# Slot bias carried inside the logits weights, slot sums moved to ScalarE and GpSimd, and the first combine weights split among the experts

## The chip, the cores and the metric

One core of a Trainium2 chip runs the whole program. The metric is the device time in microseconds from start to end of one execution, as a median of several runs. Matrices are multiplied by TensorE (PE, with its weight load PEld), the other engines are VectorE (DVE), ScalarE (ACT), GpSimd (POOL) and SyncE (SP), which issues most of the DMAs.

## What is computed

The reference, cut to what matters:

```python
h = patches @ W.T + b                       # 32 images, 36 patches each, 256 channels
h = concatenate([h, txt], axis=1)           # 36 + 77 = 113 tokens an image, 3616 in all
h = h + attention(layernorm(h))             # 16 heads of 16, rotary q and k, no scale or shift in the norm
x = layernorm(h)                            # mean 0 over the 256 channels
logits = (x @ phi_w.T + phi_b).reshape(t, z, 64, 32)      # 64 experts, 32 slots each: 2048 columns
D, C = softmax(logits, axis=3), softmax(logits, axis=2)   # dispatch and combine weights
X = einsum('tznp,tzd->npd', D, x)           # slot sums over all tokens
X = tanh(normalise(clip(X)))
Y = einsum('npd,ndH->npH', X, expert_w) + expert_b
out = h + einsum('tznp,npH->tzH', C, Y)
```

All is float32. Products that need care are made as three products of a high part and a low part: `hi*hi + hi*lo + lo*hi`.

## The kernel before

The program has three parts, one after the other, with a barrier of all engines between them.

**`embed`** multiplies 9 tiles of 128 patches by the patch weights on PE. Meanwhile ACT loads the weights of the later parts, and ACT and POOL split them into high and low parts (L126, L133): `wqk`, `wv`, `wo`, and last and largest `phi`, the slot weights (128 x 4096 elements), of whose low part DVE makes one half (L170). DVE also makes `bias_rows` from the slot bias, broadcast to 64 partitions: the bias in row 0, its low part in row 32, zeros elsewhere (L152 to L165).

**`attend`** goes over the 32 images as a software pipeline. Each engine runs `step(b)` for b = -3 to 33: the step normalises image b+3, projects b+2, turns b+1, scores b, and finishes b-1 and b-2. On POOL a step is the reciprocal standard deviation of the next image (L383, L385) and the sums that finish the rotary turn (L395). ACT's step ends with `xt_hi` of the next image (L447). SP loads `h_in` ahead and stores `h2`.

**`slots`** goes over 29 tiles of tokens (one of 32 rows, then 28 of 128), `step(t)` for t = -2 to 28: t up to 4 written out, 5 to 20 in a loop of 8 steps, the rest written out. What matters of a step, engine by engine:

- PE: turns `xn` of tile t+1 (L1068), makes two units of slot sums (`add_products`, L1092: for a group of four tiles, two blocks of 128 slots a unit) in `p_sum`, turns the combine weights of tile t-1 in four quarters (L1083), and makes the logits of tile t+1 in four banks of 512 columns: a bias product of `bias_ones` and `bias_rows` (L1115) and six products (L1118). In steps 5 and later the units come first and the banks are woven between the quarters; in steps up to 4 all four banks come before the units.
- DVE: per bank of the logits a maximum (L811) and a subtraction (L816), the sum of the combine weights of tile t-1 (L800), `xt_lo` (L828), the combine maximum (L839), the end of the norm (L784), the dispatch sum (L845), and then `keep_sum`: the two units of `p_sum` are copied (first group, L792) or added (L794) into `xacc`.
- ACT: copies the four banks to `comb` (L1004), takes the exponentials of `disp` and `comb` (L989), and copies the turned quarters out of PSUM (L978).
- POOL: the deviation of a later tile (L922, L924), two subtractions on `comb` that wait for L839 (L929), the scaling of `disp` (L933), which waits for L845's reciprocal, and the scaling of `comb` of the same tile (L937), which waits for L800's reciprocal, made by DVE one step later.

After the last tile PE makes eight more units (`products`), DVE adds them and normalises (`gather`, `scale`), ACT takes tanh, PE turns the blocks and applies the experts (L1167), DVE adds the expert bias (L879), ACT and POOL split the result (L1031, L951). Then `combine` runs over the 29 tiles: the stored combine weights are split (ACT L1057, DVE L904) and multiplied in 48 products a tile (L1200). The first combine product waits for `lo` of tile 0.

Of the kernel before, what the change touches and what calls it, by code (L numbers as in the profile page):

```python
# [29 lines left out]
KC = C // 128  # L30
# [46 lines left out]
def embed(nc, patches, wt, bias_row, emb, loads, identity, ident, slot_bias_row, bias_rows, bias_ones):  # L77
# [4 lines left out]
    with ExitStack() as ctx:  # L82
# [7 lines left out]
        slot_raw, slot_hi = sb("slot_raw", [64, E]), sb("slot_hi", [64, E], F32R)  # L90
# [3 lines left out]
        ident_in, slot_in = sem("ident_in"), sem("slot_in")  # L94
        slot_zero_ok, slot_hi_ok, slot_ok = sem("slot_zero_ok"), sem("slot_hi_ok"), sem("slot_ok")
        raw_in = [sem(f"raw_in{n}") for n in range(len(loads))]
        hi_done, lo_done, half_done = sem("hi_done"), sem("lo_done"), sem("half_done")
# [30 lines left out]
        @block.gpsimd  # L128
        def _(pool):
            for n, (_, hi, lo) in enumerate(loads):  # L130
                pool.wait_ge(hi_done, n + 1)
                part = slice(0, KC // 2) if n == len(loads) - 1 else slice(0, KC)
                nc.gpsimd.tensor_tensor(lo[:, part], raw[n][:, part], hi[:, part].bitcast(F32),  # L133
                                        ALU.subtract).then_inc(lo_done, 1)
            pool.wait_ge(lo_done, len(loads))
# [15 lines left out]
        def _(dve):  # L151
            nc.vector.memset(bias_rows[:].bitcast(F32), 0.0)  # L152
            nc.vector.memset(bias_ones[:].bitcast(F32), 1.0).then_inc(slot_zero_ok, 1)
            dve.wait_ge(b_in, 16)
            for t in range(tiles):
                dve.wait_ge(mm_done, t + 1)
                nc.vector.tensor_tensor(emb_sb[:, t], acc[t % BANKS][:], bias[:], ALU.add).then_inc(emb_ready, 1)
                if t == tiles - 3:

                    dve.wait_ge(slot_in, 16)  # L160
                    nc.vector.tensor_copy(slot_hi[:], slot_raw[:]).then_inc(slot_hi_ok, 1)
                    dve.wait_ge(slot_hi_ok, 1)
                    dve.wait_ge(slot_zero_ok, 1)
                    nc.vector.tensor_copy(bias_rows[0:1], slot_raw[0:1]).then_inc(slot_ok, 1)
                    nc.vector.tensor_tensor(bias_rows[32:33], slot_raw[32:33], slot_hi[32:33].bitcast(F32),  # L165
                                            ALU.subtract).then_inc(slot_ok, 1)
            dve.wait_ge(slot_ok, 2)
            dve.wait_ge(hi_done, len(loads))
            _, hi, lo = loads[-1]
# [1105 lines left out]
```

## Time and profile before

| | |
|---|---|
| median of 3 runs | 1049.57 us (1048.29 to 1051.22) |
| the profiled execution, its own time | 1050.74 us |
| its span | 1049.0 us |
| mean granted TensorE clock | 0.958 |
| PE busy | 953.9 us (91%) |
| DVE busy | 752.7 us (72%) |
| ACT busy | 483.3 us (46%) |
| POOL busy | 459.6 us (44%) |

| stretch, us from the span's start | what runs | length |
|---|---|---|
| 0 to 42 | embed | 42 |
| 42 to 348 | attend | 306 |
| 348 to 443 | slots, steps -2 to 4 | 95 |
| 443 to 814 | slots, steps 5 to 28 | 371 |
| 814 to 876 | last sums and experts | 62 |
| 876 to 1049 | combine | 173 |

The profile is of one execution. A busy time is the sum of an engine's instructions; the idle time before an instruction is put down to the engine that released it last. Ends of matmuls are modelled, their starts are recorded.

### The profile page before, as it was taken

To read this page: it belongs to the slowest core of one execution; us is meant where nothing else is said; L and a number is where in the kernel's file an instruction comes from. 1 tells how busy PE (TensorE), PEld (TensorE's weight loads), DVE (VectorE), ACT (ScalarE), POOL (GpSimd) and SP (SyncE) were. 2 spreads that over 40 slices of the span, in tenths; PEclk is the share of its full clock that TensorE was granted. 3 is DMA by queue.
4 is the path that set the end of the run, shared out by engine and by line. 5 is a ranking of instruction groups with operands and counts; after the bars stand their busy time and mean duration, and the time that the engine had idled before them with its cause. 6 is when DMAs were issued, how large, how long until landed. Compare 5 with 4: busy or idle time off the path is not lost.

```text
span 1049.0 us, 22748 instructions
## 1 busy us (share of the span) xinstructions
PE 953.9 (91%) x8338; PEld 809.2 (77%) x8338; DVE 752.7 (72%) x1095; ACT 483.3 (46%) x768; POOL 459.6 (44%) x375
## 2 busy tenths in 40 slices
PE   7389999999997558799999999999998997999997
PEld 6278888887885346688887888888887756999997
DVE  1746767667663398899998999999998553544442
ACT  1145555555553144565565565566556233333331
POOL 0422222222220077687786787777777341010100
PEclk9689999999998788999999999999999998999999
DMA  9201111111110402223323223323325894776660
GB/s 303 73 21 36 42 42 42 40 41 40 41 33 29 103 10 56 58 79 92 80 61 88 68 67 90 82 60 86 91 62 180 318 410 145 236 224 240 220 201 23
DMA packets 97688, 110.42 MB, mean 105 GB/s; under 512 B 12148, under 2 KB 88980, under 8 KB 91684
## 3 DMA queue, kind: packets, MB, share of 16 engines
q1 hardware_dynamic: 95460, 102.31, 31.7%
q10 hardware_dynamic: 800, 3.74, 1.0%
q0 software_dynamic: 1376, 3.70, 0.9%
q8 instruction: 29, 0.48, 0.2%
q14 instruction: 23, 0.19, 0.1%
HBM read 71.51 MB, written 38.21 MB: 105 GB/s over the span
## 4 chain that ended last, share of the span: by engine, by line
DVE 26%; PE 24%; issue 11%; POOL 3%; ACT 2%; DVEq 0%; DMA 0%; POOLq 0%; ACTq 0%
PE slots_p_turn L1200 15%; DVE slots_dmax L811 6%; DVE slots_csum L800 6%; DVE slots_dsum L845 5%; PE slots_p_sum L1092 3%; DVE slots_disp L816 3%; PE slots_logits L1118 3%; DVE xacc L794 3%; ACT slots_comb L1004 1%; PE slots_logits L1167 1%; POOL slots_comb L929 1%; POOL slots_disp L933 1%; DVE slots_xn L784 1%; DVE slots_xt_lo L828 1%; DVE slots_cmax L839 1%
## 5 line engine op out<-in xcount | busy, mean ns | idle before, releaser
L1092 PE MATMUL slots_p_sum<-slots_x,slots_disp 128*128 128x256 f32 (+1 forms) x928 | 208.1, 382 | 6.1 <-POOL slots_disp L933 6.1
L1092 PEld LDWEIGHTS slots_p_sum<-slots_x,slots_disp 128*128 128x128 f32 (+1 forms) x928 | 174.6, 191 | 31.3 <-POOL slots_disp L933 4.7
L937 POOL TENSOR_TENSOR slots_comb<-slots_comb,slots_csum 128x2048 f32<-128x2048 f32 (+1 forms) x29 | 105.0, 3619 | 66.0 <-DVE slots_csum L802 66.0
L929 POOL TENSOR_TENSOR slots_comb<-slots_comb,slots_cmax 128x1024 f32<-128x1024 f32 (+1 forms) x58 | 112.0, 1949 | 44.1 <-DVE slots_cmax L839 44.1
L933 POOL TENSOR_TENSOR slots_disp<-slots_disp,slots_dsum 128x2048 f32<-128x2048 f32 (+1 forms) x29 | 105.8, 3647 | 0.0
L1004 ACT ACTIVATE slots_comb<-slots_logits 128x512 f32<-128x512 f32 (+1 forms) x116 | 66.1, 598 | 85.3 <-DVE slots_disp L816 85.3
L816 DVE TENSOR_TENSOR slots_disp<-slots_logits,slots_dmax 128x512 f32<-128x512 f32 (+1 forms) x116 | 80.2, 691 | 5.9 <-issue 1.9
L964 POOL DMA_DIRECT2D out<-slots_o x29 | 15.9, 548 | 156.3 <-DVE slots_o L899 156.3
L395 POOL TENSOR_TENSOR attend_stack<-attend_rope_a,attend_rope_b 113x256 f32<-113x256 f32 x64 | 45.3, 729 | 88.9 <-DVE attend_rope_b L350 88.9
L978 ACT ACTIVATE slots_ct<-slots_p_turn 128x512 f32<-128x512 f32 (+1 forms) x116 | 64.1, 580 | 38.7 <-PE slots_p_turn L1083 38.6
L811 DVE TENSOR_REDUCE slots_dmax<-slots_logits 128x16 f32<-128x512 f32 (+1 forms) x116 | 78.8, 679 | 3.3 <-PE slots_logits L1118 1.8
L989 ACT ACTIVATE slots_comb<-slots_comb 128x1024 f32<-128x1024 f32 (+1 forms) x58 | 61.5, 1060 | 33.4 <-POOL slots_comb L929 33.3
L1118 PE MATMUL slots_logits<-phi_hi,slots_xt_hi 128*128 128x512 f32 (+1 forms) x232 | 75.6, 408 | 0.0
L1118 PE MATMUL slots_logits<-phi_hi,slots_xt_lo 128*128 128x512 f32 (+1 forms) x232 | 75.3, 407 | 0.0
L1118 PE MATMUL slots_logits<-phi_lo,slots_xt_hi 128*128 128x512 f32 (+1 forms) x232 | 74.9, 405 | 0.0
L311 DVE TENSOR_REDUCE attend_stack<-attend_p_score 113x16 f32<-113x1808 f32 x32 | 65.4, 2043 | 13.2 <-PE attend_p_score L459 13.2
L1115 PE MATMUL slots_logits<-bias_rows,bias_ones 128*128 128x512 f32 (+1 forms) x116 | 54.4, 469 | 19.3 <-DVE slots_xt_lo L828 18.2
L409 ACT ACTIVATE attend_prob_t<-attend_p_score 113x904 f32<-113x904 f32 x64 | 55.7, 923 | 28.7 <-PE attend_p_score L468 28.7
L800 DVE TENSOR_REDUCE slots_csum<-slots_comb 128x32 f32<-128x2048 f32 (+1 forms) x29 | 66.0, 2277 | 3.3 <-ACT slots_comb L989 3.3
L839 DVE TENSOR_REDUCE slots_cmax<-slots_comb 128x32 f32<-128x2048 f32 (+1 forms) x29 | 66.3, 2286 | 2.8 <-ACT slots_comb L1004 1.3
L1083 PE MATMUL slots_p_turn<-ident,slots_comb 128*128 128x128 f32 (+1 forms) x464 | 63.7, 272 | 2.6 <-POOL slots_comb L937 1.5
L845 DVE TENSOR_REDUCE slots_dsum<-slots_disp 128x64 f32<-128x2048 f32 (+1 forms) x29 | 66.1, 2279 | 0.0
(132 smaller groups left out, 1973.6 us busy)
## 6 DMA issues: line engine op xcount, KB each, us to landing
combine_t<-slots_ct SPq DMA_DIRECT2D x224, 128.0 KB, 2.4
slots_comb<-combine_t SPq DMA_DIRECT2D x14, 1024.0 KB, 5.6
slots_ct<-combine_t SPq DMA_DIRECT2D x14, 1024.0 KB, 5.8
expert_w<-wexp SPq DMA_DIRECT2D x8, 1024.0 KB, 9.1
slots_disp<-wexp SPq DMA_DIRECT2D x8, 1024.0 KB, 13.4
h<-attend_h_out SPq DMA_DIRECT2D x32, 113.0 KB
slots_h_t<-h SPq DMA_DIRECT2D x28, 128.0 KB, 2.2
slots_x<-h SPq DMA_DIRECT2D x28, 128.0 KB, 2.0
```

The costliest lines, as they stand in the source:

```text
L800: nc.vector.reduce_sum(csum[0:rows, 0], comb[par % 2][0:rows], AX_X).then_inc(csum_ok, 1)
L811: nc.vector.reduce_max(dmax[0:rows, bank(b)], logits[0:rows, bank(b), :], AX_X).then_inc(dmax_ok, 1)
L816: nc.vector.tensor_tensor(disp[c % RING][0:rows, bank(b), :], logits[0:rows, bank(b), :], dmax[0:rows, bank(b)].unsqueeze(2).broadcast_to( ...
L839: nc.vector.reduce_max(cmax[0:rows], comb[c % 2][0:rows], AX_X).then_inc(cmax_ok, 1)
L845: nc.vector.reduce_sum(dsum[0:rows, 0], disp[c % RING][0:rows], AX_X).then_inc(dsum_ok, 1)
L929: nc.gpsimd.tensor_tensor(m, m, cmax[0:rows, shalf(i)].unsqueeze(2).broadcast_to([rows, SLOTS // 2, EXPERTS]), ALU.subtract).then_inc(csub ...
L933: nc.gpsimd.tensor_tensor(d, d, dsum[0:rows, 1].unsqueeze(2).broadcast_to([rows, EXPERTS, SLOTS]), ALU.mult).then_inc(disp_ok, 1)
L937: nc.gpsimd.tensor_tensor(m, m, csum[0:rows, 1].unsqueeze(2).broadcast_to([rows, SLOTS, EXPERTS]), ALU.mult).then_inc(comb_ok, 1)
L1004: nc.scalar.activation(comb[c % 2][0:rows, :, bank(b)], logits[0:rows, bank(b), :].rearrange("p n s -> p s n"), ACT.Copy).then_inc(copied_ ...
L1092: last = nc.tensor.matmul(p_sum[u % 2][:, i, :], disp[d][0:rows].rearrange("p n s -> p (n s)")[:, 128 * e:128 * e + 128], x[d][0:rows], st ...
L1118: last = nc.tensor.matmul(out_b, a[:, k, 0:nrows], wt[:, k, cols], start=False, stop=i == 2 and k == KC - 1)
L1200: last = nc.tensor.matmul(p_o[c % 2][0:rows], a[c % 2][:, e, 0:rows], part[:, e, :], start=k == 0, stop=k == 3 * EB - 1)
```

## The change

It has four parts.

1. **Slot bias.** Since a row of `xn` has mean zero, the product with the slot weights stays the same when the weights of channel 0 are taken from those of all other channels; channel 0 then isn't needed. The kernel takes channels 1 to 255 so, and puts a constant one in column 256 of `xn` and the slot bias in the last weight row. The bias products (L1115) and all that made `bias_rows` go away.
2. **Split of the slot weights.** The load of `phi` moves from embed to the start of attend, on SP's queue: 2 MB in three DMAs, and channel 0's row broadcast to 128 partitions (1 MB). POOL waits for all four (in step -2) and then does a subtraction and a low part on each of four pieces of 1024 columns, in steps -2 to 2; ACT makes the high parts at the end of steps -1 to 2.
3. **Slot sums.** `keep_sum` leaves DVE. ACT copies `p_sum` to `part_sum` (or to `xacc` in the first group), POOL adds it to `xacc` in two new instructions a step from step 5 on. ACT's copy of the first unit stands after bank 1's copy in steps 5 and later, and after bank 3's copy in steps 1 to 4; that of the second unit after the second quarter.
4. **Combine's first weights.** The splits of combine's tiles 0 and 1 move from behind the experts to between the last of them.

```diff
@@ embed: loads of phi and slot bias, and their splits, removed (cut) @@
-        slot_raw, slot_hi = sb("slot_raw", [64, E]), sb("slot_hi", [64, E], F32R)
-            act.dma_start(slot_raw[:], slot_bias_row.broadcast_to([64, E])).then_inc(slot_in, 16)
-            nc.vector.tensor_tensor(lo[:, KC // 2:KC], raw[-1][:, KC // 2:KC], hi[:, KC // 2:KC].bitcast(F32),
-                                    ALU.subtract).then_inc(half_done, 1)
@@ attend, SP @@
+            sp.dma_start(phi_raw[0:127], phi[1:128]).then_inc(phi_in, 16)
+            sp.dma_start(phi_raw[127:128, 0], phi[0:1, 1]).then_inc(phi_in, 16)
+            sp.dma_start(phi_raw[127:128, 1], slot_bias).then_inc(phi_in, 16)
+            sp.dma_start(phi_first[:], phi[0:1, 0].broadcast_to([128, E])).then_inc(phi_in, 16)
@@ attend, POOL, end of a step @@
+                if isinstance(b, int) and -2 <= b < PIECES - 2:
+                    pool.wait_ge(phi_in, 64)
...
+                    nc.gpsimd.tensor_tensor(piece(phi_raw, i)[rows], piece(phi_raw, i)[rows], phi_first[rows, part],
+                                            ALU.subtract).then_inc(phi_sub_ok, 1)
+                if isinstance(b, int) and -1 <= b < PIECES - 1:
+                    pool.wait_ge(phi_hi_ok, b + 2)
+                    nc.gpsimd.tensor_tensor(piece(phi_lo, b + 1), piece(phi_raw, b + 1), piece(phi_hi, b + 1).bitcast(F32),
+                                            ALU.subtract).then_inc(phi_lo_ok, 1)
@@ attend, ACT, end of a step @@
+                if isinstance(b, int) and -1 <= b < PIECES - 1:
+                    act.wait_ge(phi_sub_ok, b + 2)
+                    nc.scalar.activation(piece(phi_hi, b + 1), piece(phi_raw, b + 1), ACT.Copy).then_inc(phi_hi_ok, 1)
@@ slots, DVE: step @@
-                for s, u in sums(t, c):
-                    keep_sum(s, u)
@@ slots, POOL: step @@
+            def add_sum(s, u):
+                pool.wait_ge(acc_ok, val(s + 1))
+                pool.wait_ge(add_ok, val(s - UNITS + 1))
+                part = xacc[:, 2 * u:2 * u + 2, :]
+                nc.gpsimd.tensor_tensor(part, part, part_sum[u % 2][:], ALU.add).then_inc(add_ok, 1)
...
+                units = sums(t, c) if not static(t) or t > TG else []
...
+                if units:
+                    add_sum(*units[0])
                 if live:
                     pool.wait_ge(cmax_ok, val(t + 1))
...
+                    if units:
+                        add_sum(*units[1])
                     pool.wait_ge(crec_ok, val(t + 1))
@@ slots, ACT: step @@
+            def keep_sum(s, u):
+                act.wait_ge(sum_ok, val(s + 1))
+                to = xacc[:, 2 * u:2 * u + 2, :]
+                if not static(s) or s >= UNITS:
+                    act.wait_ge(add_ok, val(s - 1))
+                    to = part_sum[u % 2][:]
+                nc.scalar.activation(to, p_sum[u % 2][:], ACT.Copy).then_inc(acc_ok, 1)
...
+                        if units and b == (NB - 1 if static(t) and t <= TG else 1):
+                            keep_sum(*units[0])
                     exp_half(disp[c % RING], nhalf, dsub_ok, 2, dexp_ok, 0)
                     exp_half(disp[c % RING], nhalf, dsub_ok, 2, dexp_ok, 1)
                 if weights:
                     keep_quarter(t - 1, (c + 1) % 2, half(-1), 0)
                     keep_quarter(t - 1, (c + 1) % 2, half(-1), 1)
+                    keep_sum(*units[1])
@@ slots, ACT: among the experts @@
                 if m + 2 < UNITS:
                     tanh(m + 2)
+                else:
+                    high_weights(m + 2 - UNITS, 0, m + 2 - UNITS, 128)
@@ slots, DVE: among the experts @@
+            scale(UNITS - 1)
+            for i in range(2 * UNITS - 8, EB):
+                add_bias(i)
+                if i >= EB - 4 and i % 2:
+                    low_weights((i - EB + 3) // 2, (i - EB + 3) // 2, 128)
@@ slots, PE @@
-                for k in range(KC):
-                    last = nc.tensor.transpose(p_turn[0][:, k, 0:nrows], xn[(c + 1) % 2][0:nrows, 128 * k:128 * k + 128],
+                    last = nc.tensor.transpose(p_turn[0][:, k, 0:nrows], xn[(c + 1) % 2][0:nrows, 128 * k + 1:128 * k + 129],
...
-                    nc.tensor.matmul(out_b, bias_ones[:, 0:nrows], bias_rows[:, cols], start=True, stop=False)
```

## Rows read from the trace of the kernel before

**Rows 1.** Busy time by stretch: length; PE, PEld, DVE, ACT, POOL; clock, DMA, GB/s.
```profile
0.00:33.00 33.00, 25.39 (x108) 21.45 (x108) 11.58 (x12) 5.14 (x5) 6.95 (x7) 1.00 0.81 277
...
610.69:626.03 15.34, 15.34 (x79) 13.11 (x78) 14.99 (x20) 8.81 (x15) 11.79 (x7) 1.00 0.29 77
```
**Rows 2.** Timeline of DVE: start, duration, instruction, idle before; sum of combine weights.
```profile
373.37 2.26 DVE L800 TENSOR_REDUCE slots_csum<-slots_comb 32x32 f32<-32x2048 f32 x1
...
390.12 2.27 DVE L800 TENSOR_REDUCE slots_csum<-slots_comb 128x32 f32<-128x2048 f32 x1
...
442.63 2.29 DVE L800 TENSOR_REDUCE slots_csum<-slots_comb 128x32 f32<-128x2048 f32 x1 [0.73 <-ACT slots_comb L989]
```
**Rows 3.** Chain of work that ended last: start, length, work.
```profile
798.63 2.29 DVE slots_csum L800
...
814.33 12.03 PE slots_p_sum L1092 x48
```
**Rows 4.** Timeline of PE over one step in the loop.
```profile
614.42 0.38 PE L1068 MATMUL slots_p_turn<-ident,slots_xn 128*128 128x128 f32 x2
...
622.34 0.47 PE L1115 MATMUL slots_logits<-bias_rows,bias_ones 128*128 128x512 f32 x1
622.65 0.63 PE L1118 MATMUL slots_logits<-phi_hi,slots_xt_hi 128*128 128x512 f32 x2
623.12 0.63 PE L1118 MATMUL slots_logits<-phi_lo,slots_xt_hi 128*128 128x512 f32 x2
...
629.84 0.38 PE L1068 MATMUL slots_p_turn<-ident,slots_xn 128*128 128x128 f32 x2
```
**Rows 5.** Timeline of DVE in the same step.
```profile
611.07 1.22 DVE L794 TENSOR_TENSOR xacc<-slots_p_sum,xacc 128x512 f32<-128x512 f32 x2
```
**Rows 6.** Timeline of POOL in the same step.
```profile
617.60 3.62 POOL L937 TENSOR_TENSOR slots_comb<-slots_comb,slots_csum 128x2048 f32<-128x2048 f32 x1 [2.00 <-DVE slots_csum L802]
...
623.48 3.86 POOL L929 TENSOR_TENSOR slots_comb<-slots_comb,slots_cmax 128x1024 f32<-128x1024 f32 x2 [1.48 <-DVE slots_cmax L839]
```
**Rows 7.** Timeline of the embedding's end, POOL and DVE.
```profile
24.35 2.35 POOL L133 TENSOR_TENSOR wqk_lo<-embed_raw,wqk_hi 128x1024 fp32r<-128x1024 f32 x1 [23.78 <-ACT wqk_hi L126]
26.67 2.24 POOL L133 TENSOR_TENSOR wv_lo<-embed_raw,wv_hi 128x512 fp32r<-128x512 f32 x1
...
34.96 6.62 DVE L170 TENSOR_TENSOR phi_lo<-embed_raw,phi_hi 128x2048 fp32r<-128x2048 f32 x1 [0.91 <-ACT phi_hi L126]
```
**Rows 8.** Groups of instructions by line: busy, mean ns, idle before.
```profile
L1004 ACT ACTIVATE slots_comb<-slots_logits 128x512 f32<-128x512 f32 (+1 forms) x116 | 66.1, 598 | 85.3 <-DVE slots_disp L816 85.3
...
L989 ACT ACTIVATE slots_disp<-slots_disp 128x1024 f32<-128x1024 f32 (+1 forms) x58 | 57.9, 1049 | 0.0
```
**Rows 9.** Timeline: embed's products, attend's first load; then a load's landing (DMA issues).
```profile
9.96 20.99 PE L146 MATMUL embed_acc<-embed_wt_sb,embed_px 128*128 128x256 f32 x96 [0.48 <-DMA embed_px<-patches]
...
42.08 0.39 SPq L267 DMA_DIRECT2D attend_h_in<-emb  x1
...
slots_h_t<-h SPq DMA_DIRECT2D x28, 128.0 KB, 2.2
```
**Rows 10.** Timeline of attend's step 0, POOL and PE.
```profile
74.74 0.19 POOL L383 TENSOR_TENSOR attend_mv<-attend_mv,attend_eps 113x1 f32<-113x1 f32 x1 [2.82 <-DVE attend_mv L336]
...
77.08 0.36 PE L551 MATMUL attend_p_row<-ident,attend_xn 113*128 113x113 f32 x2
```
**Rows 11.** Timeline of slots' step 2, PE and DVE.
```profile
393.11 0.79 PE L1115 MATMUL slots_logits<-bias_rows,bias_ones 128*128 128x512 f32 x1 [3.84 <-DVE slots_xt_lo L828]
...
401.74 1.99 PE L1092 MATMUL slots_p_sum<-slots_x,slots_disp 32*128 32x256 f32 x8
...
398.89 2.28 DVE L845 TENSOR_REDUCE slots_dsum<-slots_disp 128x64 f32<-128x2048 f32 x1
```
**Rows 12.** Timeline of the experts' end, PE.
```profile
869.90 1.07 PE L1167 MATMUL slots_logits<-slots_disp,slots_xn 128*32 128x256 f32 x16 [1.73 <-issue]
876.08 3.78 PE L1200 MATMUL slots_p_turn<-y_hi,slots_hi 128*128 128x256 f32 x16 [5.11 <-DVE slots_lo L904]
```

More of the change, by code:

```diff
@@ L588, in slots @@
         h_t = [sb(f"h_t{i}", [128, C]) for i in range(2)]
-        xn = [sb(f"xn{i}", [128, C]) for i in range(2)]
+        xn = [sb(f"xn{i}", [128, C + 1]) for i in range(2)]
         x = [sb(f"x{i}", [128, C]) for i in range(RING)]
@@ L603, in slots @@
         e_power = sb("e_power", [128, EB])
+        part_sum = [sb(f"part_sum{i}", [128, 2, C]) for i in range(2)]
         logits = pb("logits", [128, EXPERTS, SLOTS])
@@ L611, in slots @@
         WRING = len(w)
-        xst = [t[:].rearrange("p (k c) -> p k c", k=KC) for t in xn]
+        xst = [t[:, 0:C].rearrange("p (k c) -> p k c", k=KC) for t in xn]
         y = [t[:] for t in h_t]
@@ L770, in _ @@
             nc.vector.memset(e_power[:], -0.5)
+            for i in range(2):
+                nc.vector.memset(xn[i][:, C:C + 1], 1.0)
             nc.vector.memset(power[:], -0.5).then_inc(consts, 1)
@@ L889, in _ @@
                     add_bias(2 * u - 7)
-            scale(UNITS - 1)
-            for i in range(2 * UNITS - 8, EB):
-                add_bias(i)
             def finish(n, turn, c, rows):
@@ L899, in finish, with low_weights @@
                 nc.vector.tensor_tensor(o[c % 2][0:rows], p_o[c % 2][0:rows], h_res[c][0:rows], ALU.add).then_inc(o_ok, 1)
-            def low_part(n, turn, c, rows):
+            def low_weights(n, c, rows):
                 dve.wait_ge(hi_ok, val(n + 1))
@@ L905, in low_part @@
                                         ALU.subtract).then_inc(lo_ok, 1)
+            scale(UNITS - 1)
[3 more added lines that the diff above has]
+                    low_weights((i - EB + 3) // 2, (i - EB + 3) // 2, 128)
+            def low_part(n, turn, c, rows):
+                if not static(n) or n >= 2:
+                    low_weights(n, c, rows)
                 if not static(n) or n >= 1:
@@ L984, in step @@
                 weights = not static(t) or t >= 1
+                units = sums(t, c)
                 def exp_half(buf, cut, before, per, done, i):
@@ L994, in step @@
                         act.wait_ge(sum_ok, val(summed_before(t, c)))
-                    nc.scalar.activation(x[c % RING][0:rows], xn[c % 2][0:rows], ACT.Copy).then_inc(kept_ok, 1)
+                    nc.scalar.activation(x[c % RING][0:rows], xn[c % 2][0:rows, 0:C], ACT.Copy).then_inc(kept_ok, 1)
                 if nxt:
@@ L1031, in high_part, with high_weights @@
                 nc.scalar.activation(y_hi[:, i], y[i % 2], ACT.Copy).then_inc(y_hi_ok, 1)
+            def high_weights(n, turn, c, rows):
+                act.wait_ge(w_ld[c], val(16 * (turn + 1)))
+                if static(n) and n < 2:
+                    act.wait_ge(sum_ok, FINAL + UNITS)
+                wait_for(act, mm_ok, n - 1)
+                nc.scalar.activation(hi[c % 2][:, :, 0:rows], raw[c][:, :, 0:rows], ACT.Copy).then_inc(hi_ok, 1)
             tanh(0)
@@ L1048, in _, with later_weights @@
                     tanh(m + 2)
+                else:
+                    high_weights(m + 2 - UNITS, 0, m + 2 - UNITS, 128)
             high_part(EB - 2)
             high_part(EB - 1)
-            def high_weights(n, turn, c, rows):
-                act.wait_ge(w_ld[c], val(16 * (turn + 1)))
-                if static(n) and n < 2:
-                    act.wait_ge(sum_ok, FINAL + UNITS)
-                wait_for(act, mm_ok, n - 1)
-                nc.scalar.activation(hi[c % 2][:, :, 0:rows], raw[c][:, :, 0:rows], ACT.Copy).then_inc(hi_ok, 1)
-            turns(act, high_weights)
+            def later_weights(n, turn, c, rows):
+                if not static(n) or n >= 2:
+                    high_weights(n, turn, c, rows)
+            turns(act, later_weights)
         @block.tensor
```

73 lines of the change are left out of this document (31 added, 42 removed).

## The prediction

> **What bounds the kernel now.** I read the busy times by stretch first. In a step of the tile loop [rows 1] PE is busy for all of 15.34 us and DVE for 14.99, POOL for 11.79, ACT for 8.81. The page's chain of work runs through DVE there: the sum of the combine weights, L800, begins at 442.63 in step 5 and at 798.63 in step 28 [rows 2, 3], which is 356.0 us for 23 periods, 15.34 each and 3.2 once where the loop turns back. PE's timeline then shows that it is just as full: from one turn of `xn` to the next are 629.84 - 614.42 = 15.42 us [rows 4], with no idle time in between. So two engines bound the 24 steps together, and whoever takes work from only one gains nothing. The steps before (t up to 4) are another case: there DVE waits at the end of each step for ACT (0.73 us before L800 [rows 2]), and the chain runs xt_lo, four banks of logits, the first sums, the quarters, ACT, L800. Period 17.5 us, from (442.63 - 390.12)/3. The embedding ends with DVE's half of `phi_lo` at 34.96 + 6.62 = 41.58 [rows 7], 10.6 us after PE's last product (9.96 + 20.99 = 30.95 [rows 9]). The combine stage is PE alone, and the change leaves its 48 products a tile.
>
> **Embedding: minus 7.9.** What is left at the end are the last addition (0.42) and store. Products end at 30.95, the addition at about 31.5, the store is issued and lands 2.2 us later, as loads of the same 128 KB do [rows 9]: 33.7, and 0.5 for the barrier (41.58 to attend's first DMA at 42.08 [rows 9]) gives 34.2 in place of 42.08.
>
> **Attention: plus 2.5 (0 to 5).** The load of 3 MB stands in SP's queue between the loads of the second and the third image, and POOL waits for it in step -2. At the 277 GB/s of the embedding [rows 1] it needs some 11 us, so it lands about 14 us into attend. Step -2's rotary sums are ahead of the wait; behind it stands the deviation of the next image, and PE turns that image only some 17 us in, so the wait itself is all but hidden. The pieces are not quite. Each costs POOL two instructions of 1024 columns, 2.35 us each by the nearest row [rows 7]. In step 0 POOL's rotary sums end at 74.74 - 2.82 = 71.92; with 4.7 behind them POOL is free at 76.6, where the deviation L383 began at 74.74. It comes 1.9 later, the normalised rows at about 77.9, and PE wanted them at 77.08 [rows 10]: 0.8 us. The same in step 1, less in -1. ACT's four copies of 1024 (1.05 each [rows 8]) stand ahead of the copy that PE's next transposes need, some 0.5 each. Sum 2.5.
>
> **First logits: minus 1.5.** Four bias products on the chain of step -1: between 4 x 0.235 [rows 4] and 4 x 0.79 (the length of the first at the lower clock [rows 11]), 0.9 to 3.2; since only the first banks run at that clock, 1.5.
>
> **Steps 1 to 4: plus 8.8 (2 to 11).** Here the change puts a wait in a bad place. ACT's copy of the first unit stands behind bank 3's copy, and in these steps PE makes all four banks of the next tile's logits before the units. Behind the waiting ACT are both exponentials of `disp`, and DVE's sum L845 waits for those. In numbers, step 2 [rows 11]: logits from 393.11 to 401.74 (8.63 us for 28 products); without the four bias products 24/28 of it, 7.4, so the units begin at 400.5. The first is half of 1.99 and a drain, done at 401.65. ACT's copy 0.6, two exponentials 2.1 [rows 8]: 404.35. L845 starts then in place of 398.89, ends at 406.6, its reciprocal at 407.1. Then come the two banks' maxima and subtractions, 2.6, and L800 at 409.8, where it was at 407.9. Period 19.5 in place of 17.5; the first one, 390.12 - 373.37 = 16.75, grows by 2.8. Sum 3 x 2.0 + 2.8 = 8.8. The bias products save nothing here, since they are inside the new wait.
>
> **Steps 5 to 28: minus 19 (-26 to -3).** Each engine's new period:
> - PE loses four bias products. One start to the next is 0.31 (622.34 to 622.65) and 0.235 for the others (622.65 to 623.12, two products [rows 4]). The extra 0.08 may belong to the change from transposes to products and stay. So between 4 x 0.235 = 0.94 and 1.19 go: 14.25 to 14.5.
> - DVE loses 1.22 [rows 5] and a wait of 0.05: 14.07.
> - ACT gets two copies out of PSUM of 0.6 [rows 8]: 10.0. The first one waits for PE's first unit, and behind it stand the copies of banks 2 and 3, which release L839. The unit is done 3.5 us after PE's turn, about when DVE has bank 2 ready, so DVE's phase locks behind PE's. As DVE has 0.4 to spare, this makes no period longer by itself.
> - POOL gets two additions of 512 columns, both operands in SBUF. No row has that alone: 2.35 for 1024 from above and 2.24 for 512 next to busy DVE [rows 7]; and POOL's own broadcast form costs 3.86/2 for 1024 [rows 6]. I take 1.25 (half of 2.35 and a little), between 1.1 and 2.24. Period 11.79 + 2.5 = 14.3, with its issue gaps 14.4. They fit into the idle 2.00 and 1.48 us ahead of L937 and L929 [rows 6], which in the shorter period are all used up.
>
> So three engines come to 14.1 to 14.5, and I take 14.5: 23 x 14.5 = 333.5. From L800 of step 5 to the first product behind the loop were 814.33 - 442.63 = 371.7. Now: PE's units of step 5 begin 1.15 after L800 (POOL's last `disp` is later, as above), 333.5, 2.5 at the turn of the loop, and 15.3 from step 28's units to that product (13.8 before; the lock on PE costs 1.5). Sum 352.5, so minus 19.2.
>
> A row bears on POOL's part. DVE's `phi_lo` half took 6.62 us beside POOL's, and POOL's 512 columns 2.24 beside DVE's casts [rows 7]: they block each other whole, not by shares. The Trainium skill (SBUF — State Buffer, Who interferes with whom) has the rule that a DVE instruction with two SBUF inputs, or in a two-port mode such as `tensor_scalar` can take, and a GpSimd instruction lock each other out. By that rule L784 is the one DVE instruction of the step that can meet the new additions; the reductions can't. By the places that the sum gives them the first addition ends just as L784 begins, so by the rule's worst case L784 waits in each step, and the time is that of the second rival below; without it, it is my sum.
>
> **Experts to combine: minus 5.0 (-5.1 to -2).** PE idles 5.11 us before combine's first product [rows 12], for ACT's and DVE's splits. With these made between the experts, it starts as the last expert ends. What they delay is covered: ACT's 1.9 us hold the turned blocks, but PE waits 1.73 us for the last expert's weights anyway [rows 12], and DVE's second split is needed only a tile later.
>
> **Sum.** -7.9 + 2.5 - 1.5 + 8.8 - 19.2 - 5.0 = -22.3. The profiled execution took 1050.74, so 1028.4 by its own time; it is 1.2 above the median of the runs, and against that 1049.57 - 22.3 = 1027.3. I say 1027.
>
> **The rivals.**
> - **The early wait is hidden or smaller.** If ACT's copies came earlier than I place them, steps 1 to 4 would take 17.5 or lose their bias products as well (-1.2 each): 1027 - 9 to 14 = about 1015. Against it: the order of PE's instructions is plain. 0.10.
> - **The engines don't interlock so well.** Three engines within 0.4 us of one another, each waiting for the others, may settle at 15.0: 23 x 0.5 more, 1039. For it: L784 can be held by POOL's addition for up to 1.2 us, and DVE has 0.4 to spare. 0.17.
> - **It gains nothing in the loop.** Period 15.34 as now: 1027 + 19 = 1046, on the edge of no change. 0.05.
> - **Slower: POOL becomes the bound.** If each addition takes 2.24 us, as the 512 columns beside DVE did, POOL's period is 11.79 + 4.5 + 0.1 = 16.4 and the loop 23 x 1.9 = 44 longer than my sum: 1071. It decides from 1.9 us an addition on, where the total passes 1049.57 + 3 (a loop period of 15.6). Against it: what ran beside the 2.24 were casts, and the reductions that run beside L937 and L929 leave them at their length. 0.07.
> - Forecast 0.61.
>
> **How the numbers follow.** My own case spans 1020 to 1034 (loop period 14.25 to 14.8, attention 0 to 5, early steps 6 to 11). To hold 8 in 10 the range takes in most of the 15.0 case and the hidden early wait: 1013 to 1042. A difference under 0.3% (3.1 us) is no change for a measurement of this kernel: faster 0.88, within it 0.05, slower 0.07.
>
> **What would show it.** After the change the trace should have attend's first DMA at about 34; PE's L551 in steps 0 and 1 of attend waiting for the normalised rows by less than 1 us; L800 in steps 1 to 4 every 19.5 us with DVE idle before L845, released by ACT; in the loop 14.5 us a step, PE with no idle time, POOL busy above 95%, POOL's additions at 1.1 to 1.3 us; combine's first product less than 0.5 us behind the last expert. I would be wrong if POOL's additions are longer than 1.5 us, if L784 is found stretched to above 1 us in each step, or if L845 in step 2 isn't late.

## The result and the profile after

The changed kernel took 1109.46 us (median of 4 runs, 1107.16 to 1113.3) against 1049.03 of the kernel before: ratio 1.058, 95% interval 1.054 to 1.061. It is 60 us slower; the prediction was 1027 and faster. The profiled execution of after spans 1111.6 us, that of before 1049.0. A whole kernel's time further down that has no ratio beside it is of a single run and has no interval.

| stage, from its first event to the next one's (us) | before | after | difference | predicted |
|---|---|---|---|---|
| embedding, to attend's first load | 42.1 | 34.5 | -7.6 | -7.9 |
| attend, to slots' first statistics | 307.6 | 387.9 | **+80.3** | +2.5 |
| first logits, to the combine sum of step 1 | 23.6 | 23.6 | 0.0 | -1.5 |
| steps 1 to 4, four periods of that sum | 69.3 | 82.3 | +13.0 | +8.8 |
| steps 5 to 28, on to the last such sum | 369.2 | 352.4 | -16.7 | -19.2, with the line below |
| from there to combine's first product | 64.3 | 60.5 | -3.8 | -5.0 |
| combine | 172.9 | 170.4 | -2.5 | 0 |
| span | 1049.0 | 1111.6 | +62.6 | -22.3 |

Six of the seven lines come out within 4.2 us of the forecast. One is off by 78, and it alone turns the sign. It shows at once in SyncE's queue of after (start, duration, issuing instruction). Attend's first load, at 42.08 before [rows 9], is now at 34.48, as forecast; then one issue lasts 36.6 us:

```profile
34.48 0.39 SPq L251 DMA_DIRECT2D attend_h_in<-emb  x1
...
37.03 1.24 SPq L258 DMA_DIRECT2D attend_phi_raw<-phi  x1
38.32 36.63 SPq L259 DMA_DIRECT2D attend_phi_raw<-phi  x1
74.99 0.57 SPq L260 DMA_DIRECT2D attend_phi_raw<-phi_b  x1
75.60 1.14 SPq L261 DMA_DIRECT2D attend_phi_first<-phi  x1
76.79 4.21 SPq L251 DMA_DIRECT2D attend_h_in<-emb  x1
...
125.80 0.30 SPq L251 DMA_DIRECT2D attend_h_in<-emb  x1
```

L258 is the load of 127 rows of `phi`, 2032 KB. The stretches of after (same columns as in [rows 1]) say how it went:

```profile
45.00:75.00 30.00, 5.61 (x20) 4.39 (x20) 0.43 (x2) 1.48 (x3) 1.41 (x2) 0.56 0.06 27
75.00:80.00 5.00, 0.00 (x0) 0.00 (x0) 0.00 (x0) 0.00 (x0) 0.00 (x0) 0.50 0.54 208
80.00:100.00 20.00, 0.00 (x0) 0.00 (x0) 0.00 (x0) 0.00 (x0) 0.00 (x0) 0.50 0.11 40
100.00:120.00 20.00, 0.00 (x0) 0.00 (x0) 0.00 (x0) 0.00 (x0) 0.00 (x0) 0.50 0.06 27
```

The last two columns are the mean busy share of the 16 DMA engines and GB/s. 0.06 is 1/16: one engine is busy and fifteen are idle, at 27 GB/s, where the embedding had 0.81 and 277 GB/s [rows 1]. 2032 KB at 27 GB/s are 77 us: from 38 to 115. With the shares of the loads queued behind it the one engine stays busy until 122. No compute engine works from 75 to 120, and both waits that end it are for data of this queue, DVE's for the third image's tokens, POOL's for the last of the `phi` loads:

```profile
45.05 0.38 DVE L351 TENSOR_TENSOR attend_xt_lo<-attend_p_row,attend_xt_hi 128x226 fp32r<-128x226 f32 x1
122.59 0.43 DVE L322 BATCH_NORM_STATS2 attend_stats<-attend_h_in 113x6 f32<-113x256 f32 x1 [77.16 <-DMA attend_h_in<-txt]
...
122.21 2.34 POOL L392 TENSOR_TENSOR attend_phi_raw<-attend_phi_raw,attend_phi_first 128x1024 f32<-128x1024 f32 x1 [75.58 <-DMA attend_phi_first<-phi]
```

The early steps are as the prediction described them, only longer. DVE in step 1 of after: the sum of `disp` waits for ACT's exponentials, and the combine sum follows 20.58 us after the last one (before: 16.75 there [rows 2]).

```profile
446.04 2.26 DVE L801 TENSOR_REDUCE slots_csum<-slots_comb 32x32 f32<-32x2048 f32 x1
...
454.47 0.41 DVE L794 TENSOR_SCALAR slots_xn<-slots_h_t,slots_mv,slots_rstd 128x256 f32<-128x256 f32 x1
461.24 2.29 DVE L846 TENSOR_REDUCE slots_dsum<-slots_disp 128x64 f32<-128x2048 f32 x1 [6.37 <-ACT slots_disp L1021]
...
466.62 2.28 DVE L801 TENSOR_REDUCE slots_csum<-slots_comb 128x32 f32<-128x2048 f32 x1
```

In the loop the step is 14.46 us by DVE's sums (PE's units begin at 663.53 and 677.98), with POOL's additions at 1.27 and 1.28; POOL is busy for 97% of the time from 560 to 800. Every fourth step is longer, 15.3, because there a new group of tiles begins and PE waits for the `disp` just made:

```profile
663.53 7.07 PE L1134 MATMUL slots_p_sum<-slots_x,slots_disp 128*128 128x256 f32 x32
...
707.68 7.17 PE L1134 MATMUL slots_p_sum<-slots_x,slots_disp 128*128 128x256 f32 x32 [0.61 <-POOL slots_disp L952]
```
```profile
664.23 1.27 POOL L930 TENSOR_TENSOR xacc<-xacc,slots_part_sum 128x512 f32<-128x512 f32 x1
665.45 3.62 POOL L958 TENSOR_TENSOR slots_comb<-slots_comb,slots_csum 128x2048 f32<-128x2048 f32 x1
...
669.82 1.28 POOL L930 TENSOR_TENSOR xacc<-xacc,slots_part_sum 128x512 f32<-128x512 f32 x1
671.16 3.87 POOL L948 TENSOR_TENSOR slots_comb<-slots_comb,slots_cmax 128x1024 f32<-128x1024 f32 x2
675.00 3.65 POOL L952 TENSOR_TENSOR slots_disp<-slots_disp,slots_dsum 128x2048 f32<-128x2048 f32 x1
```

And the wait of 5.11 us ahead of combine's first product [rows 12] is 0.33:

```profile
941.22 2.03 PE L1244 MATMUL slots_p_turn<-y_hi,slots_hi 128*128 128x256 f32 x15 [0.33 <-DVE slots_lo L901]
```

### The profile page after: what moved, and what is told of

Read it like the earlier page. It is cut to its first block, busy times and chain, and to the rows that moved or that the text cites. A ratio compares the mean times of both kernels' runs of the same rounds, so it can differ in the third digit from the quotient of the medians.

```text
span 1111.6 us, 22694 instructions
## 1 busy us (share of the span) xinstructions
PE 945.5 (85%) x8222; PEld 799.2 (72%) x8222; DVE 703.6 (63%) x1035; ACT 508.5 (46%) x827; POOL 534.5 (48%) x431
## 4 chain that ended last, share of the span: by engine, by line
PE 48%; DVE 5%; POOL 5%; issue 2%; ACT 2%; DMA 0%; POOLq 0%; ACTq 0%; DVEq 0%
PE slots_p_sum L1134 17%; PE slots_p_turn L1244 14%; PE slots_logits L1159 13%; PE slots_p_turn L1125 3%; POOL slots_disp L952 2%; POOL slots_comb L948 2%; DVE slots_cmax L840 1%; PE slots_logits L1211 1%; DVE slots_dsum L846 1%; DVE slots_csum L801 1%; ACT slots_disp L1021 1%; POOL y_lo L972 1%; DVE slots_dmax L812 1%; ACT slots_comb L1036 1%; DVE slots_disp L817 0%
## 5 line engine op out<-in xcount | busy, mean ns | idle before, releaser
L1134 PE MATMUL slots_p_sum<-slots_x,slots_disp 128*128 128x256 f32 (+1 forms) x928 | 211.6, 386 | 11.7 <-POOL slots_disp L952 11.7
L1159 PE MATMUL slots_logits<-phi_hi,slots_xt_hi 128*128 128x512 f32 (+1 forms) x232 | 84.9, 450 | 24.5 <-DVE slots_xt_lo L829 23.4
L558 PE MATMUL attend_p_row<-ident,attend_xn 113*128 113x113 f32 x64 | 12.5, 279 | 81.5 <-DVE attend_xn L327 81.5
L840 DVE TENSOR_REDUCE slots_cmax<-slots_comb 128x32 f32<-128x2048 f32 (+1 forms) x29 | 66.3, 2286 | 16.8 <-ACT slots_comb L1036 16.5
L1036 ACT ACTIVATE slots_comb<-slots_logits 128x512 f32<-128x512 f32 (+1 forms) x116 | 63.7, 597 | 20.4 <-DVE slots_disp L817 20.1
L1125 PE MATMUL slots_p_turn<-ident,slots_comb 128*128 128x128 f32 (+1 forms) x464 | 66.1, 279 | 5.2 <-ACT slots_ct L999 5.2
L1125 PEld LDWEIGHTS slots_p_turn<-ident,slots_comb 128*128 128x128 f32 (+1 forms) x464 | 56.5, 144 | 16.4 <-ACT slots_ct L999 6.3
```

The source lines that it names most:

```text
L840: nc.vector.reduce_max(cmax[0:rows], comb[c % 2][0:rows], AX_X).then_inc(cmax_ok, 1)
L1036: nc.scalar.activation(comb[c % 2][0:rows, :, bank(b)], logits[0:rows, bank(b), :].rearrange("p n s -> p s n"), ACT.Copy).then_inc(copied_ ...
L1125: last = nc.tensor.transpose(p_turn[q % 2][:, i, 0:rows], weights[:, 128 * e:128 * e + 128], ident[0:rows, 0:rows])
L1134: last = nc.tensor.matmul(p_sum[u % 2][:, i, :], disp[d][0:rows].rearrange("p n s -> p (n s)")[:, 128 * e:128 * e + 128], x[d][0:rows], st ...
L1159: last = nc.tensor.matmul(out_b, a[:, k, 0:nrows], wt[:, k, cols], start=i == 0 and k == 0, stop=i == 2 and k == KC - 1)
```

## The experiments

### One load, split in two

The theory from the traces: a count of 127 rows, a prime number, puts the whole load on one DMA engine. The first kernel changes the rows of that load and nothing else, the second asks by which rule the engines are counted.

```diff
-            sp.dma_start(phi_raw[0:127], phi[1:128]).then_inc(phi_in, 16)
+            sp.dma_start(phi_raw[0:112], phi[1:113]).then_inc(phi_in, 16)
+            sp.dma_start(phi_raw[112:127], phi[113:128]).then_inc(phi_in, 16)
...
-                    pool.wait_ge(phi_in, 64)
+                    pool.wait_ge(phi_in, 80)
```

> Edit: the load of rows 0 to 126 of the slot weights' tile is issued as two, of 112 and of 15 rows; all else as in the changed kernel. One-engine theory (127 rows, a prime count, go through one of the 16 DMA engines at about 27 GB/s, 2032 KB in some 75 us; 112 and 15 rows are spread over 16 and 15): the two land within 6 to 10 us, the 75 us at a DMA share of 0.06 go, attend's 80 us of extra shrink to 2 to 9, and the time is about 1035 us (1031 to 1042), which is below the kernel before's 1049. Rival, the one-row loads or the broadcast of one row to 128 partitions are what is slow: nothing changes, 1105 to 1110. Rival, the volume (3 MB beside attend's loads): at most 3 us go, 1106 to 1110.

Measured: **1038.82 us** (ratio to before 0.9905, 0.9874 to 0.9935). The same split by 121 and 6 rows:

> Edit: the same load as two, of 121 and of 6 rows. If the count of engines is the largest divisor of the row count that is at most 16 (121 gives 11): while the 121 rows move the DMA share is about 0.69, they take some 6.5 to 10 us, and the time is that of the 112 and 15 rows within 3 us, about 1035. If only even counts or multiples of 16 are spread and an odd count is not: share 0.06 for some 72 us, time 1102 to 1108. If it is the last few rows beyond a multiple of 16 that go slow: as the 112 and 15 rows.

Measured: 1044.25 us. The stretches while the loads run, first with 112 and 15 rows, then with 121 and 6:

```profile
40.00:44.00 4.00, 3.28 (x8) 2.14 (x8) 1.86 (x6) 0.36 (x1) 0.75 (x2) 0.57 1.02 262
44.00:48.00 4.00, 2.04 (x15) 2.05 (x15) 0.71 (x3) 0.93 (x2) 1.41 (x2) 0.86 1.01 162
48.00:52.00 4.00, 2.62 (x8) 1.56 (x6) 0.00 (x0) 0.55 (x1) 0.00 (x0) 0.71 0.83 277
```
```profile
44.00:48.00 4.00, 2.21 (x15) 2.22 (x16) 0.54 (x2) 0.93 (x2) 1.41 (x2) 0.82 0.80 169
48.00:52.00 4.00, 2.45 (x7) 1.51 (x6) 0.00 (x0) 0.55 (x1) 0.00 (x0) 0.75 0.69 150
```

All sixteen engines are busy with 112 rows, and a share of 0.69 = 11/16 stands in the second from 48 to 52: 11 engines for 11 x 11 rows, as expected. So an odd count is not the trouble; a count without a divisor up to 16 is. That costs 70.6 us here (1109.46 - 1038.82). The two rivals (one-row loads, the volume alone) fall. The 0.69 is a mean, though: by single microseconds the share goes from 0.51 to 0.86 there, so it fits 11 engines and does not count them. The time with 121 rows is 5.4 us above that with 112, where at most 3 were expected.

The Trainium skill (DMA: Bandwidth & Descriptors, Why a DMA increments its semaphore by 16 and not by 1) states this rule: the number of engines is the largest one up to 16 that divides the outermost sizes of both sides, with 127 partitions giving one as its example. The shares 0.06, 0.69 and 1.0 agree with it. The prediction did not weigh it.

The split kernel still lost in attend: 314.8 us from 33.75, against 307.6. The 3 MB stand ahead of the third image's tokens in the queue, on all engines now, and DVE waited 8.21 us for those:

```profile
52.92 0.43 DVE L323 BATCH_NORM_STATS2 attend_stats<-attend_h_in 113x6 f32<-113x256 f32 x1 [8.21 <-DMA attend_h_in<-txt]
```

With 121 rows attend took 321.2, and DVE waited 12.65 us for the same tokens. That is 6.4 us more, against 5.4 between the two kernels as a whole.

### Who stops attend: the wait, the queue or the engine

Two kernels, each run once, keep the whole load of 127 rows, but make the pieces of `phi` in attend's last five steps, so that nobody waits for it early. In the second one it is issued by ScalarE, past SyncE's queue.

```diff
-                if isinstance(b, int) and -2 <= b < PIECES - 2:
-                    pool.wait_ge(phi_in, 64)
-                    i = b + 2
+                if isinstance(b, int) and BATCH - 3 <= b < BATCH + 1:
+                    pool.wait_ge(phi_in, 64)
+                    i = b + 3 - BATCH
```

> Edit: the load of 127 rows stays whole, but GpSimd and ScalarE make the pieces of the slot weights in attend's last five steps, so no engine waits for the load at attend's start. Theory A, the load holds back what is queued behind it on SyncE (the issue of the next load took 36.6 us and the tokens of step 2 were issued only at 81 us): attend's early steps still stop until about 77 us, the time stays near 1105 us (1098 to 1112). Theory B, it is GpSimd's wait for the load that stops attend, and the tokens' loads would have gone through: the time falls to about 1035 us (1030 to 1045).

Measured: 1106.8 us. Theory A held: with no one waiting for `phi`, DVE still waits 76.85 us for the third image's tokens. GpSimd's wait was not the cause. The pieces had a price of their own, though. The stop ends alike in both kernels (the third image's statistics begin 88.1 us into attend, here 87.9), but those of the seventh image begin at 126.6 in after and at 121.9 here: the early pieces cost some 4.5 us, where 2.5 had been forecast.

```diff
-            sp.dma_start(phi_raw[0:127], phi[1:128]).then_inc(phi_in, 16)
 ...
         def _(act):
+            act.dma_start(phi_raw[0:127], phi[1:128]).then_inc(phi_in, 16)
```

> Edit: the late pieces, and the load of 127 rows is issued by ScalarE instead of SyncE. If the stop is in SyncE's queue alone, the tokens' loads go on beside the slow one: no stop at attend's start, the load still takes some 75 us at a DMA share near 0.06, and the time is about 1035 us (1030 to 1045). If the busy engine delays every load that has a share on it, the tokens' loads (77 and 36 rows) land late too: some 1060 to 1105.

Measured: 1106.51 us, the second alternative, and 1.5 us beyond its far end. SyncE's queue and DVE:

```profile
36.46 41.19 SPq L257 DMA_DIRECT2D attend_sin<-rope_sin  x1
77.69 37.93 SPq L258 DMA_DIRECT2D attend_phi_raw<-phi  x1
```
```profile
46.56 0.43 DVE L321 BATCH_NORM_STATS2 attend_stats<-attend_h_in 113x6 f32<-113x256 f32 x1 [10.62 <-DMA attend_h_in<-txt]
...
54.25 0.43 DVE L321 BATCH_NORM_STATS2 attend_stats<-attend_h_in 113x6 f32<-113x256 f32 x1 [3.88 <-DMA attend_h_in<-txt]
...
116.55 0.69 DVE L334 TENSOR_TENSOR attend_rope_a<-attend_p_qk,attend_cos 113x512 f32<-113x512 f32 x1 [60.23 <-DMA attend_sin<-rope_sin]
```

Now it is the small table `sin` of 113 rows (113 is prime too) whose issue lasts 41 us and whose landing, at 116, releases DVE. Issuing from another engine's queue does not help. It does change what is held back: the tokens of the first two images (77 and 36 rows) came late, with 10.62 and 3.88 us of wait, but long before the load's end, while the table of 113 rows came only at its end. The third image's tokens were not issued before 116, since the long issues blocked SyncE. Whether issue and landing are held by one mechanism or two, and why the tokens passed and the table did not, was not separated.

### The early steps: what stands behind a waiting copy

From here on each kernel has the load in 112 and 15 rows and is compared with its 1038.82 us, unless the text says that it is built on the kernel before. The first moves ScalarE's copy of the first unit behind both exponentials in steps 1 to 4.

```diff
-                        if units and b == (NB - 1 if static(t) and t <= TG else 1):
+                        if units and b == 1 and not (static(t) and t <= TG):
                             keep_sum(*units[0])
                     exp_half(disp[c % RING], nhalf, dsub_ok, 2, dexp_ok, 0)
                     exp_half(disp[c % RING], nhalf, dsub_ok, 2, dexp_ok, 1)
+                if units and static(t) and t <= TG:
+                    keep_sum(*units[0])
```

> Edit, on top of the load in 112 and 15 rows (1038.8 us): in slots' steps 1 to 4 ScalarE copies the first unit's sum behind the two exponentials of disp instead of ahead of them. Theory, that copy (which waits for PE's four banks and the unit) holds the exponentials back and VectorE waits for them 6.3 us in each of these steps: the period of these steps falls from 20.5 us to 17 to 18.5, the loop stays at 14.67 us a step, and the time is about 1028 us (1025 to 1031). Rival, the steps are long since PE runs at the lower clock there (24 products in 8.5 us): the period stays above 20, the time 1036 to 1040.

Measured: **1024.35 us** (ratio to before 0.977, 0.975 to 0.979), 14.5 us less, and just under the expected 1025 to 1031. Steps 1 to 4 took 67.4 us, 16.9 each, against 82.3, and the loop's first step, which had still carried the wait, 14.2 against 16.6. DVE's sum of `disp` begins right behind its predecessor, and what is left is the wait for ACT's exponentials of the combine weights that before had too, 0.73 us long [rows 2]:

```profile
397.25 0.40 DVE L795 TENSOR_SCALAR slots_xn<-slots_h_t,slots_mv,slots_rstd 128x256 f32<-128x256 f32 x1
397.57 2.28 DVE L847 TENSOR_REDUCE slots_dsum<-slots_disp 128x64 f32<-128x2048 f32 x1
...
405.47 2.29 DVE L802 TENSOR_REDUCE slots_csum<-slots_comb 128x32 f32<-128x2048 f32 x1 [2.44 <-ACT slots_comb L1022]
```

### The loop: either part alone

Part 3 undone (VectorE keeps the sums, by the code of before; GpSimd's additions and ScalarE's copies are gone), then, on the kernel before, part 3 alone.

```diff
+                for s, u in sums(t, c):
+                    keep_sum(s, u)              # VectorE
...
-                        if units and b == (NB - 1 if static(t) and t <= TG else 1):
-                            keep_sum(*units[0])   # ScalarE
...
-                if units:
-                    add_sum(*units[0])            # GpSimd
```

> Edit, on top of the load in 112 and 15 rows (1038.8 us): the slot sums are kept by VectorE, as in the kernel before, so that only parts 1 and 4 and the early split of the slot weights are left. Theory, VectorE sets the step of the loop: its period goes back to about 15.3 us (24 steps by 0.67: +16), steps 1 to 4 fall back to 17 or 17.5 us (-12 to -14): about 1042 us (1038 to 1046). Rival, PE and its bias products set the loop's step, and VectorE has room: the loop stays near 14.6, and with the shorter first steps the time is about 1026 us (1023 to 1030).

Measured: 1044.36 us (ratio to before 0.9952, 0.9931 to 0.9972). The opposite edits made on the kernel before:

> Edit, on the kernel before (1047.8 us): part 3 alone, the slot sums copied by ScalarE and added by GpSimd; the bias products stay. Theory, with the four bias products PE needs about 15.1 us a step, so freeing VectorE gives 0.1 to 0.25 us a step, and steps 1 to 4 pay 3 us each: about 1056 us (1050 to 1062), the loop's period 15.1 to 15.3. Rival, VectorE alone set the step: the period falls to 14.5 to 14.7 and the time to about 1042 (1038 to 1046).

Measured: 1064.78 us in one run, 16 above before and some 3 above the expected range. The periods of the loop: 15.34 without part 3, 15.40 with part 3 alone, 15.34 before, 14.46 (14.68 on average) with both. 120 us of each loop, first part 3 undone, then part 3 alone:

```profile
600.00:720.00 120.00, 115.14 (x579) 97.22 (x579) 117.27 (x147) 70.40 (x111) 92.19 (x48) 0.99 0.29 75
```
```profile
600.00:720.00 120.00, 120.00 (x610) 102.28 (x609) 108.58 (x132) 77.00 (x125) 110.64 (x63) 1.00 0.28 74
```

With part 3 undone PE is idle for 5 of 120 us and DVE is full (117.27, at the 15.34 us of before); with part 3 alone DVE has 11 us to spare and PE none. Each part frees an engine that is not the only bound, and gains nothing in the loop; together they give 16.7 us. I had put PE's step with the bias products at 15.1 and it is 15.40, as [rows 4] (15.42) already said. As steps 1 to 4 lose 12.5 us in it (81.8 for 69.3), part 3 alone is a loss.

### Combine's first weights

Part 4 undone: both first splits behind the last expert, as before.

```diff
-                else:
-                    high_weights(m + 2 - UNITS, 0, m + 2 - UNITS, 128)
...
-            turns(act, later_weights)
+            turns(act, high_weights)
```

> Edit, on top of the load in 112 and 15 rows (1038.8 us): part 4 undone, both of combine's first splits behind the last expert. Theory: ScalarE's and VectorE's split stand between the last expert and combine's first product again, 4 to 5 us: about 1043 us (1041 to 1045), the slot stage's time up to the last expert unchanged. Rival, ScalarE and VectorE have no room among the experts and part 4 only moves the work: within 1.5 us of 1038.8.

Measured: 1046.65 us in one run, 7.8 more, where 1041 to 1045 was expected. From the last combine sum to combine's first product it took 65.0 us against 60.5: 4.6, as expected. Combine itself took 3.9 more, though the edit changes nothing there but the first tile: VectorE's output additions follow one another at 5.75 us on average against 5.63, in all 28 tiles alike. `keep_on_dve`, which doesn't touch this stage, shows 5.75 too, and the kernel before 5.68. So a combine tile varies by 2% between the profiled executions for a reason that no run here isolates (each kernel has only one, so it may be the program or the execution), and differences of up to 4 us in that stage are no edit's.

### Loads spread over the steps, and stores that are no prime

On top of ScalarE's later copy, the loads of `phi` are cut into column pieces, one behind the tokens' loads in each of SyncE's first four steps (the one-row loads and the broadcast follow in the fifth), and the pieces are made in the last five steps, as in the late pieces above. These are two edits in one kernel.

```diff
+                if isinstance(b, int) and -3 <= b < PIECES - 3:
+                    i = b + 3
+                    part = slice(i % 2 * (E // 2), (i % 2 + 1) * (E // 2))
+                    sp.dma_start(phi_raw[0:112, i // 2, part], phi[1:113, i // 2, part]).then_inc(phi_in, 16)
+                    sp.dma_start(phi_raw[112:127, i // 2, part], phi[113:128, i // 2, part]).then_inc(phi_in, 16)
```

> Edit, on top of the 112 and 15 rows and ScalarE's later copy (1024.4 us): the slot weights are loaded in four pieces of 448 and 60 KB, one in each of SyncE's first four steps of attend behind the tokens' loads, and GpSimd and ScalarE make the pieces in attend's last five steps. Theory: the 3 MB ahead of the tokens of attend's third step held them back (VectorE waited 8.2 us for them) and the pieces made in the first steps held GpSimd's small work back (3 us waits of VectorE, twice): together the 6.5 us that attend still had above the kernel before. They go: 1018 us (1015 to 1020). Rival, the clock and not the loads (PE at 0.6 to 0.7 in attend's first 25 us): no change, 1023 to 1026.

Measured: **1013.82 us** (0.9673, 0.9649 to 0.9698), below the expected 1015 to 1020. Attend took 307.2 us, as before the change, 7.8 less than in the kernel that it is built on; how much of it is the loads' place and how much the pieces' was not separated. The other 2.7 us lie in stages that the edit gives no reason for: the experts (58.3 us to combine's first product, for 60.8) and combine (170.0 for 172.0) were shorter, steps 1 to 4 longer (69.3 for 67.4).

The 113 rows of attend's output are prime as well. Each store as 112 rows and 1 row, first on this kernel, then alone on the kernel before:

```diff
-                    sp.dma_start(h2[bass.ds(val((b - 2) * T), T), :], h_out[par][:]).then_inc(h2_out[par], 16)
+                    sp.dma_start(h2[bass.ds(val((b - 2) * T), 112), :], h_out[par][0:112]).then_inc(h2_out[par], 16)
+                    sp.dma_start(h2[bass.ds(val((b - 2) * T + 112), 1), :], h_out[par][112:113]).then_inc(h2_out[par], 16)
```

> Edit, on top of the later load: each store of attend's 113 rows of h2 is issued as 112 rows and 1 row. Theory, 113 is a prime count as 127 is, so each store goes through one engine; at attend's end the wait for the last store (7.4 us in the kernel before) falls to about 3 us: 4 to 5 us less, about 1013 us (1011 to 1016). Rival, the 7.4 us are the fixed time of a store and of the change of stage: within 1 us of the later load's time.

Measured: **1010.05 us** (0.9638, 0.962 to 0.9657), the best of all, 3.6% below the kernel before. That is 3.8 us less, a little under the 4 to 5 expected; the time lies below its range of 1011 to 1016 because the kernel under it lay below its own.

> Edit, on the kernel before (about 1048.5 us) and nothing else: each store of attend's 113 rows is issued as 112 rows and 1 row. Theory, a store of 113 rows goes through one DMA engine, and only the last one is waited for: SyncE's wait at attend's end falls from 7.4 to about 1.2 us, attend itself stays as long, the time falls by 4 to 6 us to 1043 or 1044. Rival, the store is slow only where other transfers share its engine: within 1.5 us of the kernel before.

Measured: 1044.51 us (0.9956, 0.9939 to 0.9973), 4.5 less than 1049.03, within the theory's 4 to 6. In the kernel before the DMA engines' share is 0.07, at 25 GB/s, from 340 to 347, while the last stores land: one engine again. SyncE's wait at the end of attend (total, times, longest), before and with the store split alone:

```profile
SPq L294 <- DMA h<-attend_h_out: 7.4, 1, 7.4
```
```profile
SPq L295 <- DMA h<-attend_h_out: 1.4, 1, 1.4
```

31 of the 32 stores cost nothing, since nobody waits for them; the last one is on the path, and there the rule costs 6 us in the wait and 4.5 in the total. Attend was 6.2 us shorter in that profile; the slots' stretch up to step 4 gave 2.4 back (24.8 and 70.5 us for 23.6 and 69.3), where PE stayed longer at the lower clock: the burst of 28 products in step -1 took 9.25 us for 8.14.

## Why the prediction was wrong

- **Embedding, -7.9.** Right: attend's first load at 34.48, forecast 34.2.
- **Attention, +2.5, range 0 to 5.** This step failed, and with it the sign. "At the 277 GB/s of the embedding it needs some 11 us": the rate came from loads of 128 rows and was given to a load of 127. It measured 27 GB/s, and the load that was to be in about 14 us into attend held up its readers until 88 us in. The bound on the unknown was drawn from rows of another shape, and no rival asked what the new load's shape does. The trace of before held the same shape in small: stores of 113 rows with 7.4 us of wait at attend's end, whose price I had not read. Behind it stands a second, smaller error: I looked at who waits for `phi` (POOL) and not at what is queued behind it. With all engines the 3 MB were in 18.8 us into attend, not 14, and held back the third image's tokens by 8.2 us of wait; the wait was not "all but hidden", and attend was 7.2 us longer. POOL's piece of 2.35 us was right (2.34 to 2.38), but what the pieces cost the stage was not: some 4.5 us for 2.5, by the comparison with the late pieces.
- **First logits, -1.5.** Not there (23.6 and 23.6 us): the burst of step -1 took 8.23 us for 24 products and 8.14 for 28 before. See the next point.
- **Steps 1 to 4, +8.8, range 2 to 11.** The mechanism was right, wait by wait, and moving the copy took it away. The size was 13.0, above the range, by one term: the 24 products of logits were put at 24/28 of 8.63 = 7.4 us and took 8.50 from 469.62 to the first unit (8.44 to 8.55 in the other steps). PE's timeline in step 2 shows why (two products a line):

```profile
469.62 1.22 PE L1159 MATMUL slots_logits<-phi_hi,slots_xt_hi 128*128 128x512 f32 x2 [5.67 <-DVE slots_xt_lo L829]
...
474.05 1.05 PE L1159 MATMUL slots_logits<-phi_hi,slots_xt_lo 128*128 128x512 f32 x2
474.91 0.95 PE L1159 MATMUL slots_logits<-phi_hi,slots_xt_hi 128*128 128x512 f32 x2
475.70 0.63 PE L1159 MATMUL slots_logits<-phi_lo,slots_xt_hi 128*128 128x512 f32 x2
```

  After 5.67 us of idling the first twelve products run at the lower level of the clock, 1.05 us a pair, and the rest at 0.63. The granted clock is 0.50 up to 475 and 1.00 from 476 on. So products taken out of such a burst are not sure to be saved at its mean rate. What sets how long the lower level lasts stays open. The idle time ahead was 3.84 us before [rows 11] and 5.67 here, but it does not decide alone: behind the same 3.18 us of idling these 24 products took 7.08 us in the kernel with ScalarE's later copy alone (7.08 to 7.34 in steps 2 to 4, as forecast) and 8.35 in the kernel with the later loads.
- **Steps 5 to 28, -19.2.** Right in kind and nearly in size: 14.46 us a step (forecast 14.5), POOL's additions 1.27 (1.25), POOL busy for 97%, no stretching of the DVE instruction that could have met them (0.41 us), and the slower rival did not come. The rule on the shared port was hardly tried: the additions overlap that instruction by 0.1 us at most. Between the forecast's own ends, L800 of step 5 and the first product behind the loop, 371.7 us became 355.0, against 352.5. The 2.5 us that are missing are a balance: step 5 took 16.5 us, since it still carried the early wait, and every fourth step 15.2 by PE's units, where PE waits 0.61 us for the `disp` just made, together some 6 us above an even 14.46; the 2.5 put at the turn of the loop were not there. I had one period for all steps.
- **Experts to combine, -5.0.** It was -3.8, and 4.6 in the experiment that undid it.
- **The rivals.** All four moved the time by 12 to 44 us through the length of a step already in the sum, and the slower one was tied to POOL. None asked what would happen if the one new transfer was slow. With that term right, at 7, the sum would have been -18 by the forecast's own other terms; the split kernel measured -10, the difference being mainly the early steps (4.2), the first logits (1.5) and the loop (2.5).

## What to carry to other kernels

Before a transfer is added or reshaped, look at the number of rows it has: 127 and 113 rows each went through one of 16 DMA engines, and taking 112 of them as one transfer and the rest as another gave 70 us and 4.5 us. Ask of each new transfer both who waits for it and what is queued behind it on every engine that it touches, and put large, unhurried loads behind the small urgent ones (7.8 us here, together with making their pieces later). Where two engines are full together, edits that free either one are worth nothing alone (15.34 and 15.40 us a step) and 0.9 us a step together (0.7 on average over the loop); and a copy that waits must not stand ahead of work that others wait for (14.5 us).

## What the chip showed that I had not expected

- One busy DMA engine holds back loads of other queues, and not all alike: with the 127 rows issued by ScalarE, SyncE's issue of a table of 113 rows lasted 41.19 us and the table came at 116, while loads of 77 and 36 rows came at 46 and 54.
- An issue can block its engine: 36.63 us for a one-row load, where the issues ahead of it took 0.26 to 1.24.
- The busy share of the DMA engines shows how many work: 0.06 for 127 rows, about 0.69 for 121, 1.0 for 112.
- The same 24 products of step -1 took 6.86 us in one kernel and 8.28 in another, by how long PE stayed at the granted clock of 0.50. The stretch from the first statistics to the combine sum of step 1 took 22.3 us in the one and 23.7 in the other.
- Without any edit there, combine's tile took 5.63 us in some kernels' profiles, 5.68 in others and 5.75 in two, all at full clock. This stays open.
